# Two layer norms' inverse roots in one GpSimd instruction, and the first norm's statistics one step ahead

## The chip, the cores and the metric

The kernel runs on one core of a Trainium2 chip. The metric is the device time of one execution in microseconds; three executions of the kernel before took 194.07 to 194.81 us, median 194.49. Profiled executions come with a trace of every engine: PE (TensorE, matmuls; PEld is its loading of weights), DVE (VectorE), ACT (ScalarE), POOL (GpSimd) and SP (which issues DMAs).

## The reference

A layer of pre-norm linear attention with gate and depthwise convolution, and a small FFN in fp8, over x of shape (32, 256, 128):

```python
def _layernorm(x, axis=-1, eps=1e-05):
    m = jnp.mean(x, axis=axis, keepdims=True)
    v = jnp.var(x, axis=axis, keepdims=True)
    return (x - m) / jnp.sqrt(v + eps)

# attention on h = _layernorm(x):
q, k, v = h @ Wq.T, h @ Wk.T, h @ Wv.T      # 8 heads of 16; rope on q and k
kv   = einsum('bshd,bshe->bhde', k, v); ksum = k.sum(1); vsum = v.sum(1)
o    = (q.kv * scale + vsum) / (q.ksum * scale + seq_len) + conv5(v) + lepe_b
x    = x + (o * (h @ Wg.T)) @ Wo.T
# FFN on h2 = _layernorm(x):
y    = fp8(bf16(h2) / s_in) @ fp8(kernel / s_k) * (s_in * s_k)
out  = x + (y.astype(bf16) + bias)
```

What the change touches is the 1 / sqrt(v + eps) of both norms, which is computed on POOL as (v + eps) to the power of −0.5.

## The kernel before, in words

The 32 sequences are handled as U = 16 units of two sequences (W = 512 tokens, four tiles of 128). The kernel is a software pipeline over steps t = 0 .. 20, written out by hand: every engine has a loop over t, and in each step it works on several units at once, LN1 of unit t, the projections of unit t−1, attention of unit t−2, output projection and LN2's statistics of unit t−3, LN2's normalisation and the FFN of unit t−4. LAG = 4 is that distance. Each engine executes its list strictly in order; semaphores (wait_ge) tie the engines together.

The lists per step are:

- SP: load_x(t+1) into one of NX = 4 buffers, which from unit 4 on waits until the residual of the unit that had the buffer is done (x2_done); then store(t−4). Ahead of the loop stand the loads of x(0), the rope tables, x(1) and seven small constants.
- PE: project_qk(t−2, 1), project_v(t−1), transpose_t1(t−3), sum_v(t−2), transpose_h2(t−4), transpose_v(t−1), project_qk(t−1, 0), ffn(t−4), project_o(t−3), key_value(t−2), transpose_q(t−2), project_g(t−2), transpose_h(t), attend(t−2). transpose_v and project_qk(·, 0) wait for ACT's move_v.
- DVE: add_lepe(t−3), stats1(t) (bn_stats of x), gate(t−3), rope(t−1, 0), the first convolution tap, residual(t−3), mask_kv(t−2), stats2(t−3), two more taps, invert and divide(t−2), rope(t−1, 1). In step 0 the projections' weights are set up behind stats1(0), in step 1 the FFN's weights (set_up_ffn).
- ACT: norm2(t−4) (L328), move_v(t−1) (L276), the fp8 quantisation (L338), var_eps1(t) (L241, L242), conv_outer and conv_middle(t−1) (L288, L297), move_y(t−4) (L347), norm1(t) (L253), move_qT(t−2) (L306), var_eps2(t−3) (L316, L317), move_hT(t) (L266).
- POOL: pow1(t) (L384, L386), add_bias(t−4) (L426), final_sum(t−4) (L435), pow2(t−3) (L395, L397), sum_outer(t−2) (L419), add_rope(t−1, 0) and add_rope(t−1, 1) (L406).

A norm thus goes through three engines: DVE's bn_stats; ACT's two instructions over 128x4, which give minus the mean (nm) and the variance plus eps (ve); POOL's pow, which gives rs, and its multiplication nm · rs (nmr); and ACT's four activations of 128x128 with scale rs and bias nmr. pow2 and its product stand between stats2 of unit t−3 and norm2 of the same unit, which is the first thing that ACT does in the next step.

Of the kernel before, what the change touches and what calls it, by code (L numbers as in the profile page):

```python
# [20 lines left out]
LAG = 4  # L21
NX = 4

# [8 lines left out]
def live(u):  # L32
    return 0 <= u < U
# [12 lines left out]
def build(nc, x, wq, wk, wv, wg, wo, lepe_w, lepe_b, ffn_w, s_in, s_k, ffn_b,  # L46
          cos_c, sin_c, ident_c, mask_c, out):
    ctx = ExitStack()
    with ctx:
# [28 lines left out]
        qn = sb("qn", [P, W])  # L78
        minus_half = sb("minus_half", [P, TPU])
        eps = sb("eps", [P, 1])  # L80
# [25 lines left out]
        st2 = sb("st2", [P, 2, BPU, 6])  # L106
        ve2 = sb("ve2", [P, 2, TPU])
        nm2 = sb("nm2", [P, 2, TPU])
        rs2 = sb("rs2", [P, 2, TPU])
        nmr2 = sb("nmr2", [P, 2, TPU])  # L110
        h2 = sb("h2", [P, 2, TPU, D], BF16)
# [33 lines left out]
        ve1_done = sem("ve1_done")  # L145
        pow1_done = sem("pow1_done")
        nmr1_done = sem("nmr1_done")
        h_done = sem("h_done")
# [27 lines left out]
        ve2_done = sem("ve2_done")  # L176
        pow2_done = sem("pow2_done")
        nmr2_done = sem("nmr2_done")
        h2_done = sem("h2_done")
# [12 lines left out]
        def _(sp):  # L192
# [16 lines left out]
            for dst, src in ((cos_t[:], cos_c), (sin_t[:], sin_c)):  # L209
                sp.dma_start(dst, src).then_inc(rope_in, 16)  # L210
            load_x(1)
            for dst, src in ((conv_w[:], lepe_w.rearrange("c a k -> c (a k)")),
                             (conv_b[:], lepe_b.rearrange("(c a) -> c a", a=1)),
                             (mask[:], mask_c),
                             (fw[:], ffn_w),
                             (fb[:], ffn_b.rearrange("(a c) -> a c", a=1).broadcast_to([P, D])),
                             (sc[:, 0:1], s_in.rearrange("(a c) -> a c", a=1).broadcast_to([P, 1])),
                             (sc[:, 1:2], s_k.rearrange("(a c) -> a c", a=1).broadcast_to([P, 1]))):
                sp.dma_start(dst, src).then_inc(c_in, 16)
            for t in range(1, U + LAG):  # L220
                load_x(t + 1)
                store(t - 4)
# [4 lines left out]
        def _(act):  # L227
            for n, w in enumerate((wq, wk, wv, wg)):
                act.dma_start(w_raw[:, n], w).then_inc(w_in, 16)
            act.wait_ge(const_set, 1)  # L230
            nc.scalar.activation(scratch[:], minus_half[:, 0:1], ACT.Identity)

            def var_eps1(u):
                if not live(u):
                    return
                s = u % 2
                act.wait_ge(stats1_done, count(u))
                if u >= 2:
                    act.wait_ge(nmr1_done, count(u, 2))
                stats = st1[:, s].rearrange("p b (a k) -> p (b a) k", k=3)  # L240
                nc.scalar.activation(nm1[:, s], stats[:, :, 1], ACT.Copy, scale=-1.0)  # L241
                nc.scalar.activation(ve1[:, s], stats[:, :, 2], ACT.Identity, scale=1.0 / D,  # L242
                                     bias=eps[:, 0:1]).then_inc(ve1_done, 1)

            def norm1(u):
                if not live(u):
                    return
                s = u % 2
                act.wait_ge(nmr1_done, count(u))
                if u >= 2:  # L250
                    act.wait_ge(hT_filled, count(u, 2))
                for t in range(TPU):
                    last = nc.scalar.activation(h[:, s, t], xs[:, u % NX, t], ACT.Identity, scale=rs1[:, s, t:t + 1],  # L253
                                                bias=nmr1[:, s, t:t + 1])
                last.then_inc(h_done, 1)
# [52 lines left out]
            def var_eps2(u):  # L308
# [7 lines left out]
                nc.scalar.activation(nm2[:, s], stats[:, :, 1], ACT.Copy, scale=-1.0)  # L316
                nc.scalar.activation(ve2[:, s], stats[:, :, 2], ACT.Identity, scale=1.0 / D,  # L317
                                     bias=eps[:, 0:1]).then_inc(ve2_done, 1)

            def norm2(u):  # L320
                if not live(u):
                    return
                s = u % 2
                act.wait_ge(nmr2_done, count(u))
                if u >= 2:
                    act.wait_ge(h2T_filled, count(u, 2))
                for t in range(TPU):
                    last = nc.scalar.activation(h2[:, s, t], x2[:, u % 3, t], ACT.Identity, scale=rs2[:, s, t:t + 1],  # L328
                                                bias=nmr2[:, s, t:t + 1])
                last.then_inc(h2_done, 1)  # L330
# [19 lines left out]
            is_small = None  # L350
            for t in range(U + LAG + 1):
                if t == 4:
# [4 lines left out]
                quantise_if_small(t - 4, is_small)  # L357
                var_eps1(t)
                conv_outer(t - 1)
                conv_middle(t - 1)  # L360
                move_y(t - 4)
                norm1(t)
                move_qT(t - 2)
                var_eps2(t - 3)
                move_hT(t)

        @block.gpsimd
        def _(pool):
# [7 lines left out]

            def pow1(u):
                if not live(u):
                    return
                s = u % 2  # L380
                pool.wait_ge(ve1_done, count(u))
                if u >= 2:
                    pool.wait_ge(h_done, count(u, 2))
                nc.gpsimd.tensor_tensor(rs1[:, s], ve1[:, s], minus_half[:], ALU.pow).then_inc(pow1_done, 1)  # L384
                pool.wait_ge(pow1_done, count(u))
                nc.gpsimd.tensor_tensor(nmr1[:, s], nm1[:, s], rs1[:, s], ALU.mult).then_inc(nmr1_done, 1)  # L386

            def pow2(u):
                if not live(u):
                    return  # L390
                s = u % 2
                pool.wait_ge(ve2_done, count(u))
                if u >= 2:
                    pool.wait_ge(h2_done, count(u, 2))
                nc.gpsimd.tensor_tensor(rs2[:, s], ve2[:, s], minus_half[:], ALU.pow).then_inc(pow2_done, 1)  # L395
                pool.wait_ge(pow2_done, count(u))
                nc.gpsimd.tensor_tensor(nmr2[:, s], nm2[:, s], rs2[:, s], ALU.mult).then_inc(nmr2_done, 1)  # L397

# [48 lines left out]
        def _(dve):  # L447
# [421 lines left out]
```

## Time and profile before

| | |
|---|---|
| median of three executions | 194.49 us |
| the profiled execution | 195.21 us |
| its span in the trace | 193.4 us |
| PE busy | 162.5 us (84%) |
| DVE busy | 151.9 us (79%) |
| POOL busy | 135.6 us (70%) |
| ACT busy | 133.2 us (69%) |
| mean granted clock of TensorE | 0.95 |

The span is the time from the first to the last instruction of the trace; the execution's time is that with what lies around it. Busy shares are averages over a fill (up to about 31 us), a plateau of equal steps and a drain (from about 163 us). The granted clock is a share of TensorE's full speed.

### The profile page before, as it was taken

How to read it: one execution, taken by the hardware profiler on the slowest of the kernel's cores; microseconds unless marked ns; L12 is line 12 of the kernel's file. 1: busy time of each engine (PE TensorE's matmuls, PEld its weight loads, DVE VectorE, ACT ScalarE, POOL GpSimd, SP SyncE). 2: the span in 40 equal slices, each digit the busy share in tenths (PEclk: the TensorE clock that was granted, in tenths of full speed). 3: DMA queues.
4: the chain of work that ended last, by engine and by line, in shares of the span. 5: the costliest groups of instructions: out<-in, count | busy, mean ns of one | idle time of the engine just before them, and what ended most of it. 6: DMA issues, size and time to landing. Idle time of an engine off the chain costs nothing.

```text
span 193.4 us, 3840 instructions
## 1 busy us (share of the span) xinstructions
PE 162.5 (84%) x1125; PEld 138.5 (72%) x1125; DVE 151.9 (79%) x308; ACT 133.2 (69%) x354; POOL 135.6 (70%) x154
## 2 busy tenths in 40 slices
PE   0467659999999999999999999999999999594220
PEld 0354549888888888989898989898989888473110
DVE  1215985999999999999999999999999989845300
ACT  3437163688888979797979797979797975435150
POOL 1213081568979897989897979898979795963704
PEclk9999988999999999999999999999999999998555
DMA  5730000010303030303030303030303020110101
GB/s 138 198 99 0 0 0 0 7 54 0 108 3 110 5 108 2 108 3 110 3 108 0 112 4 108 6 106 14 98 18 96 0 58 2 54 34 23 54 0 54
DMA packets 19078, 9.71 MB, mean 50 GB/s; under 512 B 1520, under 2 KB 18800, under 8 KB 19056
## 3 DMA queue, kind: packets, MB, share of 16 engines
q1 hardware_dynamic: 18480, 9.19, 16.6%
q10 hardware_dynamic: 576, 0.26, 0.5%
q8 instruction: 10, 0.16, 0.4%
q14 instruction: 12, 0.10, 0.2%
HBM read 5.25 MB, written 4.19 MB: 49 GB/s over the span
## 4 chain that ended last, share of the span: by engine, by line
PE 76%; issue 8%; DVE 4%; POOL 4%; ACT 4%; DMA 2%; POOLq 1%; DVEq 0%; ACTq 0%
PE bank L669 13%; PE bank L770 9%; PE bank L683 8%; PE bank L728 7%; PE p_num L741 7%; PE p_num L751 7%; PE bank L692 7%; PE bank L654 4%; PE bank L702 4%; PE bank L761 4%; PE bank L713 3%; PE bank L793 2%; DMA xs<-_attn_hidden_states_dram 2%; PE bank L781 2%; POOL qk L406 1%
## 5 line engine op out<-in xcount | busy, mean ns | idle before, releaser
L406 POOL TENSOR_TENSOR qk<-rc,rs 128x512 f32<-128x512 f32 x32 | 40.2, 1276 | 12.9 <-DVE rs L524 12.9
L540 DVE SCALAR_TENSOR_TENSOR acc<-bank,conv_w,acc 128x510 f32<-128x510 f32 (+1 forms) x48 | 35.5, 739 | 1.1 <-ACT acc L297 0.5
L328 ACT ACTIVATE h<-x,nmr,rs 128x128 bf16<-128x128 f32 x64 | 26.4, 482 | 12.1 <-POOL nmr L397 12.1
L669 PE MATMUL bank<-w_qk,hT 128*128 128x256 f32 x128 | 33.8, 387 | 0.0
L426 POOL TENSOR_TENSOR yc<-yb,fb 128x512 bf16<-128x512 bf16 x16 | 18.5, 1158 | 17.5 <-ACT yb L347 17.5
L522 DVE TENSOR_TENSOR rc<-bank,cos_t 128x512 f32<-128x512 f32 x32 | 21.9, 685 | 10.1 <-PE bank L669 10.0
L253 ACT ACTIVATE h<-xs,nmr,rs 128x128 f32<-128x128 f32 x64 | 26.3, 492 | 2.0 <-POOL nmr L386 2.0
L384 POOL TENSOR_TENSOR rs<-ve,minus_half 128x4 f32<-128x4 f32 x16 | 16.3, 1018 | 15.2 <-ACT ve L242 15.2
L669 PEld LDWEIGHTS bank<-w_qk,hT 128*128 128x128 f32 x128 | 22.4, 195 | 1.8
L524 DVE TENSOR_TENSOR rs<-bank,sin_t 128x512 f32<-128x512 f32 x32 | 21.8, 680 | 0.0
L728 PE MATMUL bank<-v,qk 128*128 128x136 f32 x128 | 17.5, 280 | 3.5 <-POOL qk L406 3.5
L419 POOL TENSOR_TENSOR acc<-acc,outer 128x508 f32<-128x508 f32 x16 | 20.3, 1268 | 0.0
L395 POOL TENSOR_TENSOR rs<-ve,minus_half 128x4 f32<-128x4 f32 x16 | 16.3, 1017 | 5.2 <-ACT ve L317 4.6
L435 POOL TENSOR_TENSOR ob<-x,yc 128x512 f32<-128x512 f32 x16 | 18.6, 1160 | 1.3
L338 ACT ACTIVATE q<-bank,rsc 128x512 fp8e4<-128x512 bf16 x16 | 11.0, 687 | 12.1 <-PE bank L781 12.1
L683 PEld LDWEIGHTS bank<-w_v,hT 128*128 128x128 f32 x128 | 17.5, 200 | 2.5 <-ACT hT L266 1.8
L770 PE MATMUL bank<-w_o,oT 128*128 128x128 f32 x128 | 19.0, 294 | 0.3
L683 PE MATMUL bank<-w_v,hT 128*128 128x128 f32 x128 | 18.0, 286 | 1.0 <-ACT hT L266 0.9
L728 PEld LDWEIGHTS bank<-v,qk 128*128 128x128 f32 x128 | 16.0, 190 | 3.9 <-issue 3.9
L751 PE MATMUL p_num<-kvs,qT 128*128 128x136 f32 x128 | 17.8, 282 | 0.0
L770 PEld LDWEIGHTS bank<-w_o,oT 128*128 128x128 f32 x128 | 16.3, 199 | 1.9 <-issue 0.6
L741 PE MATMUL p_num<-w_v,hsum 128*128 128x272 f32 x64 | 17.3, 393 | 0.0
(72 smaller groups left out, 329.4 us busy)
## 6 DMA issues: line engine op xcount, KB each, us to landing
xs<-_attn_hidden_states_dram SPq DMA_DIRECT2D x16, 256.0 KB, 2.8
out_dram<-ob SPq DMA_DIRECT2D x16, 256.0 KB, 2.3
cos_t<-in_cos_dram SPq DMA_DIRECT2D x1, 256.0 KB, 4.3
sin_t<-in_sin_dram SPq DMA_DIRECT2D x1, 256.0 KB, 5.4
mask<-in_mask_dram SPq DMA_DIRECT2D x1, 68.0 KB, 3.8
w_raw<-in_L_attn_Wq_dram ACTq DMA_DIRECT2D x1, 64.0 KB, 2.7
w_raw<-in_L_attn_Wk_dram ACTq DMA_DIRECT2D x1, 64.0 KB, 3.1
ident<-in_ident_dram SPq DMA_DIRECT2D x1, 64.0 KB, 3.2
```

Source lines behind the costliest of these rows:

```text
L253: last = nc.scalar.activation(h[:, s, t], xs[:, u % NX, t], ACT.Identity, scale=rs1[:, s, t:t + 1], bias=nmr1[:, s, t:t + 1])
L328: last = nc.scalar.activation(h2[:, s, t], x2[:, u % 3, t], ACT.Identity, scale=rs2[:, s, t:t + 1], bias=nmr2[:, s, t:t + 1])
L406: nc.gpsimd.tensor_tensor(qk[:, u % 2, j].rearrange("p q t d -> p t q d"), rc[:, j].rearrange("p a h (q d) -> p (a h) q d", q=2), rs[:, j] ...
L522: nc.vector.tensor_tensor(rc[:, j], p_qk[j], cos_t[:].rearrange("p a (h d) -> p a h d", h=2), ALU.mult)
L524: nc.vector.tensor_tensor(rs[:, j], p_qk[j][:, :, ::-1, :], sin_t[:].rearrange("p a (h d) -> p a h d", h=2), ALU.mult).then_inc(rope_done[ ...
L540: nc.vector.scalar_tensor_tensor(out=part, in0=p_vT[:, :, lo + off:hi + off], scalar=conv_w[:, k:k + 1], in1=part, op0=ALU.mult, op1=ALU.a ...
L669: last = nc.tensor.matmul(p_qk[j][:, a].rearrange("p h d -> p (h d)"), hT[:, u % 3, t * P:(t + 1) * P], w_qk[:].rearrange("p a q d -> p (a ...
L683: last = nc.tensor.matmul(p_v[:, t], hT[:, u % 3, t * P:(t + 1) * P], w_v[:, 0:D], start=True, stop=True)
L728: last = nc.tensor.matmul(p_kv[:, t // TPB], qk_tile(u, 1, t), v[:, u % 3, t], start=(t % TPB == 0), stop=(t % TPB == TPB - 1))
L741: nc.tensor.matmul(p_num[:, TPB * j:TPB * (j + 1), 0:NW], hsum[:, u % 3, j:j + 1].to_broadcast([P, P]), w_v[:].unsqueeze(1).to_broadcast([ ...
L751: last = nc.tensor.matmul(p_num[:, t, 0:NW], qT[:, u % 2, t * P:(t + 1) * P], kvs[:, u % 2, t // TPB], start=False, stop=(t % TPB == TPB - 1))
L770: last = nc.tensor.matmul(p_proj[:, t], oT[:, u % 2, t * P:(t + 1) * P], w_o[:], start=True, stop=True)
```

## The change

The four small arrays of both norms (ve, nm, rs, nmr) become arrays with a further dimension of two: index 0 is LN1, index 1 is LN2, so that for one buffer the eight values of a partition lie side by side. POOL's pow1 and pow2 become invert_roots(u), which handles LN1 of unit u and LN2 of unit u−4 in one pow over 128x8 and one multiplication over 128x8; where only one of the two units exists it takes that half (128x4). It stands where pow2 stood. LN1's statistics are moved one step forward: DVE's stats1(t+1) takes stats1(t)'s place (stats1(0) runs ahead of the loop), and ACT's var_eps1(t+1) goes behind move_qT, next to var_eps2. SP loads x(t+2) in step t instead of x(t+1), x(2) is loaded ahead of the constants, and there are five x buffers. The loops of ACT and POOL start at t = −1.

```diff
-NX = 4
+NX = 5
...
-        minus_half = sb("minus_half", [P, TPU])
+        minus_half = sb("minus_half", [P, 2, TPU])
...
-        ve1 = sb("ve1", [P, 2, TPU])
-        nm1 = sb("nm1", [P, 2, TPU])
-        rs1 = sb("rs1", [P, 2, TPU])
-        nmr1 = sb("nmr1", [P, 2, TPU])
+        ve = sb("ve", [P, 2, 2, TPU])
+        nm = sb("nm", [P, 2, 2, TPU])
+        rstd = sb("rstd", [P, 2, 2, TPU])
+        nmr = sb("nmr", [P, 2, 2, TPU])
...
             load_x(1)
+            load_x(2)
...
             for t in range(1, U + LAG):
-                load_x(t + 1)
+                load_x(t + 2)
                 store(t - 4)
...
             def var_eps1(u):
...
                 if u >= 2:
-                    act.wait_ge(nmr1_done, count(u, 2))
+                    act.wait_ge(nmr_done, u - 1)
...
             def norm1(u):
...
-                act.wait_ge(nmr1_done, count(u))
+                act.wait_ge(nmr_done, u + 1)
...
             def var_eps2(u):
...
-                if u >= 2:
-                    act.wait_ge(nmr2_done, count(u, 2))
+                act.wait_ge(nmr_done, u + LAG - 1)
...
             def norm2(u):
...
-                act.wait_ge(nmr2_done, count(u))
+                act.wait_ge(nmr_done, u + LAG + 1)
...
-            for t in range(U + LAG + 1):
+            for t in range(-1, U + LAG + 1):
...
                 quantise_if_small(t - 4, is_small)
-                var_eps1(t)
                 conv_outer(t - 1)
                 conv_middle(t - 1)
                 move_y(t - 4)
                 norm1(t)
                 move_qT(t - 2)
+                var_eps1(t + 1)
                 var_eps2(t - 3)
                 move_hT(t)
...
+            def invert_roots(u):
+                s = u % 2
+                first, second = live(u), live(u - LAG)
+                if not (first or second):
+                    return
+                k = slice(0 if first else 1, 2 if second else 1)
+                if first:
+                    pool.wait_ge(ve1_done, count(u))
+                    if u >= 2:
+                        pool.wait_ge(h_done, count(u, 2))
+                if second:
+                    pool.wait_ge(ve2_done, count(u, LAG))
+                if live(u - LAG - 2):
+                    pool.wait_ge(h2_done, count(u, LAG + 2))
+                nc.gpsimd.tensor_tensor(rstd[:, s, k], ve[:, s, k], minus_half[:, k], ALU.pow).then_inc(pow_done, 1)
+                pool.wait_ge(pow_done, u + 1)
+                nc.gpsimd.tensor_tensor(nmr[:, s, k], nm[:, s, k], rstd[:, s, k], ALU.mult).then_inc(nmr_done, 1)
...
-            for t in range(U + LAG + 1):
-                pow1(t)
+            for t in range(-1, U + LAG + 1):
                 add_bias(t - 4)
                 final_sum(t - 4)
-                pow2(t - 3)
+                invert_roots(t + 1)
                 sum_outer(t - 2)
                 add_rope(t - 1, 0)
                 add_rope(t - 1, 1)
...
             is_small = None
+            stats1(0)
+            set_up_projections()
             for t in range(U + LAG + 1):
                 add_lepe(t - 3)
-                stats1(t)
-                if t == 0:
-                    set_up_projections()
+                stats1(t + 1)
```

## Rows read from the trace of the kernel before

**Rows 1.** The page: span, and busy time by engine with its share of the span.
```profile
span 193.4 us, 3840 instructions
PE 162.5 (84%) x1125; PEld 138.5 (72%) x1125; DVE 151.9 (79%) x308; ACT 133.2 (69%) x354; POOL 135.6 (70%) x154
```

**Rows 2.** Busy time of each engine: the plateau, and one step of it.
```profile
core 0: us, PE busy (x) PEld busy (x) DVE busy (x) ACT busy (x) POOL busy (x), PEclk, DMA share, GB/s
40.66:155.06 114.40, 114.30 (x843) 100.35 (x842) 110.08 (x217) 97.51 (x266) 101.35 (x109) 1.00 0.18 52
101.95:111.49 9.54, 9.54 (x71) 8.36 (x71) 9.15 (x20) 8.14 (x23) 8.33 (x10) 1.00 0.20 57
```

**Rows 3.** Timeline of a plateau step: start us, us, engine, line, op, out<-in.
```profile
101.78 1.03 PE L669 MATMUL bank<-w_qk,hT 128*128 128x256 f32 x4
...
102.85 0.69 DVE L522 TENSOR_TENSOR rc<-bank,cos_t 128x512 f32<-128x512 f32 x1 [0.29 <-PE bank L669]
...
105.66 0.76 DVE L607 BATCH_NORM_STATS2 st<-x 128x6 f32<-128x256 f32 x2
...
106.56 0.28 ACT L317 ACTIVATE ve<-st,eps 128x4 f32<-128x4 f32 x1
...
106.92 1.02 POOL L395 TENSOR_TENSOR rs<-ve,minus_half 128x4 f32<-128x4 f32 x1
...
108.02 0.20 POOL L397 TENSOR_TENSOR nmr<-nm,rs 128x4 f32<-128x4 f32 x1
...
108.25 1.65 ACT L328 ACTIVATE h<-x,nmr,rs 128x128 bf16<-128x128 f32 x4 [0.59 <-POOL nmr L397]
...
109.81 0.57 ACT L276 ACTIVATE v<-bank 128x512 f32<-128x512 f32 x1
...
110.17 0.68 DVE L578 TENSOR_TENSOR t<-bank,acc 128x512 f32<-128x512 f32 x1
...
110.83 0.42 PEld L702 LDWEIGHTS bank<-ident,v 128*128 128x128 f32 x4
```

**Rows 4.** Who waited for whom: us in total, times, longest.
```profile
ACT h L328 <- POOL nmr L397: 12.1, 16, 1.4
```

**Rows 5.** POOL's groups by shape: busy us, mean ns, idle before.
```profile
L406 POOL TENSOR_TENSOR qk<-rc,rs 128x512 f32<-128x512 f32 x32 | 40.2, 1276 | 12.9 <-DVE rs L524 12.9
...
L384 POOL TENSOR_TENSOR rs<-ve,minus_half 128x4 f32<-128x4 f32 x16 | 16.3, 1018 | 15.2 <-ACT ve L242 15.2
L395 POOL TENSOR_TENSOR rs<-ve,minus_half 128x4 f32<-128x4 f32 x16 | 16.3, 1017 | 5.2 <-ACT ve L317 4.6
L386 POOL TENSOR_TENSOR nmr<-nm,rs 128x4 f32<-128x4 f32 x16 | 3.2, 201 | 1.3
L397 POOL TENSOR_TENSOR nmr<-nm,rs 128x4 f32<-128x4 f32 x16 | 3.2, 200 | 1.3
```

**Rows 6.** Waits again: POOL's longest.
```profile
POOL yc L426 <- ACT yb L347: 17.5, 16, 4.8
```

**Rows 7.** Timeline of the fill.
```profile
9.54 0.75 DVE L513 BATCH_NORM_STATS2 st<-xs 128x6 f32<-128x256 f32 x2
9.86 0.38 ACT L266 ACTIVATE hT<-bank 128x256 f32<-128x256 f32 x1 [1.21 <-PE bank L654]
...
10.75 2.08 PE L683 MATMUL bank<-w_v,hT 128*128 128x128 f32 x8 [0.93 <-ACT hT L266]
...
16.45 0.69 DVE L522 TENSOR_TENSOR rc<-bank,cos_t 128x512 f32<-128x512 f32 x1 [6.17 <-PE bank L669]
...
23.99 0.68 DVE L524 TENSOR_TENSOR rs<-bank,sin_t 128x512 f32<-128x512 f32 x1
...
24.75 1.27 POOL L406 TENSOR_TENSOR qk<-rc,rs 128x512 f32<-128x512 f32 x1 [5.66 <-DVE rs L524]
...
26.12 1.17 PE L728 MATMUL bank<-v,qk 128*128 128x136 f32 x8 [3.55 <-POOL qk L406]
```

**Rows 8.** Timeline of SP in the fill, and ACT's first use of a constant.
```profile
6.12 0.43 SPq L219 DMA_DIRECT2D sc<-n_L_ffn_input_scale_dram  x1
6.60 0.43 SPq L219 DMA_DIRECT2D sc<-_L_ffn_kernel_scale_dram  x1
...
14.67 0.69 ACT L288 ACTIVATE outer<-bank,conv_w 128x508 f32<-128x508 f32 x1 [0.93 <-PE bank L702]
```

**Rows 9.** Timeline of PE's weight loads in steps 2 and 3.
```profile
29.01 0.18 PEld L654 LDWEIGHTS bank<-ident,h 128*128 128x128 f32 x1 [0.87 <-ACT h L253]
29.51 0.66 PEld L654 LDWEIGHTS bank<-ident,h 128*128 128x128 f32 x3 [0.32 <-issue]
...
38.97 0.14 PEld L654 LDWEIGHTS bank<-ident,h 128*128 128x128 f32 x1 [0.34 <-ACT h L253]
```

More of the change, by code:

```diff
@@ L106, in build @@
         st2 = sb("st2", [P, 2, BPU, 6])
[L107 to L110, printed above, removed]
         h2 = sb("h2", [P, 2, TPU, D], BF16)
@@ L145, in build @@
         ve1_done = sem("ve1_done")
-        pow1_done = sem("pow1_done")
-        nmr1_done = sem("nmr1_done")
+        pow_done = sem("pow_done")
+        nmr_done = sem("nmr_done")
         h_done = sem("h_done")
@@ L230, in _ @@
             act.wait_ge(const_set, 1)
-            nc.scalar.activation(scratch[:], minus_half[:, 0:1], ACT.Identity)
+            nc.scalar.activation(scratch[:], minus_half[:, 0, 0:1], ACT.Identity)
             def var_eps1(u):
@@ L238, in var_eps1 @@
                 if u >= 2:
-                    act.wait_ge(nmr1_done, count(u, 2))
+                    act.wait_ge(nmr_done, u - 1)
                 stats = st1[:, s].rearrange("p b (a k) -> p (b a) k", k=3)
-                nc.scalar.activation(nm1[:, s], stats[:, :, 1], ACT.Copy, scale=-1.0)
-                nc.scalar.activation(ve1[:, s], stats[:, :, 2], ACT.Identity, scale=1.0 / D,
+                nc.scalar.activation(nm[:, s, 0], stats[:, :, 1], ACT.Copy, scale=-1.0)
+                nc.scalar.activation(ve[:, s, 0], stats[:, :, 2], ACT.Identity, scale=1.0 / D,
                                      bias=eps[:, 0:1]).then_inc(ve1_done, 1)
@@ L252, in norm1 @@
                 for t in range(TPU):
-                    last = nc.scalar.activation(h[:, s, t], xs[:, u % NX, t], ACT.Identity, scale=rs1[:, s, t:t + 1],
-                                                bias=nmr1[:, s, t:t + 1])
+                    last = nc.scalar.activation(h[:, s, t], xs[:, u % NX, t], ACT.Identity, scale=rstd[:, s, 0, t:t + 1],
+                                                bias=nmr[:, s, 0, t:t + 1])
                 last.then_inc(h_done, 1)
@@ L312, in var_eps2 @@
                 act.wait_ge(stats2_done, count(u))
-                if u >= 2:
-                    act.wait_ge(nmr2_done, count(u, 2))
+                act.wait_ge(nmr_done, u + LAG - 1)
                 stats = st2[:, s].rearrange("p b (a k) -> p (b a) k", k=3)
-                nc.scalar.activation(nm2[:, s], stats[:, :, 1], ACT.Copy, scale=-1.0)
-                nc.scalar.activation(ve2[:, s], stats[:, :, 2], ACT.Identity, scale=1.0 / D,
+                nc.scalar.activation(nm[:, s, 1], stats[:, :, 1], ACT.Copy, scale=-1.0)
+                nc.scalar.activation(ve[:, s, 1], stats[:, :, 2], ACT.Identity, scale=1.0 / D,
                                      bias=eps[:, 0:1]).then_inc(ve2_done, 1)
@@ L327, in norm2 @@
                 for t in range(TPU):
-                    last = nc.scalar.activation(h2[:, s, t], x2[:, u % 3, t], ACT.Identity, scale=rs2[:, s, t:t + 1],
-                                                bias=nmr2[:, s, t:t + 1])
+                    last = nc.scalar.activation(h2[:, s, t], x2[:, u % 3, t], ACT.Identity, scale=rstd[:, s, 1, t:t + 1],
+                                                bias=nmr[:, s, 1, t:t + 1])
                 last.then_inc(h2_done, 1)
@@ L375, in _ @@
             pool.wait_ge(const_set, 1)
-            def pow1(u):
-                if not live(u):
+            def invert_roots(u):
+                s = u % 2
+                first, second = live(u), live(u - LAG)
+                if not (first or second):
                     return
[L380 to L397, printed above, removed]
+                k = slice(0 if first else 1, 2 if second else 1)
[10 more added lines that the diff above has]
+                nc.gpsimd.tensor_tensor(nmr[:, s, k], nm[:, s, k], rstd[:, s, k], ALU.mult).then_inc(nmr_done, 1)
             def add_rope(u, j):
```

2 lines of the change are left out of this document (removed).

## The prediction

> **What bounds the kernel now.** The page comes first. Its busy line has PE at 84% of the span, DVE at 79%, POOL at 70% [rows 1], an average over a fill, a plateau and a drain. The busy time by stretches separates them: in the 114.40 us of the plateau PE is busy 114.30 us at full granted clock, against DVE 110.08, POOL 101.35 and ACT 97.51; a single step of 9.54 us looks the same, PE busy 9.54 of it [rows 2]. So a step costs what PE's instruction stream costs, and a microsecond taken from POOL or ACT is worth nothing there by itself. What the change can do in the plateau is make some other loop longer than 9.54 us.
>
> Which loop is the next longest? The timeline of one step shows it [rows 3]. PE finishes project_qk(·,0) (L669, 101.78 + 1.03 = 102.81). DVE then works without a gap from rope (102.85) to stats2 (105.66 + 0.76 = 106.42). ACT makes the second norm's variance (106.56 + 0.28 = 106.84), POOL takes its root (106.92) and multiplies (108.02 + 0.20 = 108.22), ACT normalises LN2 (108.25 to 109.90) and then moves v (109.81 + 0.57 = 110.38), and PE may transpose v and run the next project_qk(·,0), both of which wait for that v. PE came to transpose_v only at 110.83. The loop therefore has 110.83 − 110.38 = 0.45 us of slack, less the 0.03 us that a release takes from an end to the start that waits for it (108.22 to 108.25): 0.42. The chain of waits by pairs says that it is real: ACT's LN2 normalisation waited for POOL's nmr in all 16 steps, 12.1 us in all, up to 1.4 [rows 4]. This idle time costs nothing today, and it is where the change puts its longer instruction.
>
> **The change, part by part.**
>
> *The merged pow.* Before, a step has two pows of 128x4 (1018 and 1017 ns) and two multiplications of 128x4 (201 and 200 ns) [rows 5]. After, it has one of each over 128x8, in the place of the second pair, and so inside the loop above. What the removed first pair frees (1018 + 201 = 1.2 us of POOL) lies beside PE's work and ends nothing: POOL waited for yb (17.5 us over 16 steps) before add_bias [rows 6], and ve of LN2 was ready at 106.84, 0.08 us before the pow started, so an earlier final_sum would not start it sooner [rows 3].
>
> What does a pow over 8 elements per partition cost? No row shows one. From below: nothing more than 1018 ns, if the time is the instruction's own and not its elements'; less than nothing is excluded, since it does a superset of the work. From above: 1018 ns more, if all of it goes by elements. Between them: the multiplication of the same shape on the same engine takes 201 ns, so dispatch and access are at most that, and the other 1018 − 201 = 817 ns are pow's body. An add of 128x512 takes 1276 ns [rows 5], (1276 − 201) / 508 = 2.1 ns per further element, so elements as such are cheap; pow's body is the same code over each of them. A body done element by element costs 817 / 4 = 204 ns each, and four more cost 817. I take +0.82 us: the nearest row is that of the pow itself, whose time has no other visible home than its four elements. The multiplication grows by 4 × 2.1 ns, nothing.
>
> By the Trainium skill (GPSIMD Engine Reference, section 3.1, Elementwise — side-by-side cycle accounting) tensor_tensor costs about 2.6 cycles per element at 1.2 GHz; four more elements would be an estimated 9 ns. The adds here agree with it (2.1 ns), but it is measured on add, and the 1018 ns against 201 at equal shape show that pow doesn't follow it. The same page's section 7 (Performance pitfalls for Q7 kernels) says that a dependent fp32 chain pays 4 cycles per element on the chain, which is the form in which pow's time would grow with its elements, against this change. By the first rule the sum below is 0.8, by the second about 5.6.
>
> *What the longer pow does.* In a step nmr comes 0.82 us later. ACT's LN2 normalisation ends at 109.90 + 0.82 = 110.72, v at 111.20 instead of 110.38, and PE, ready for transpose_v at 110.83, starts it at about 111.23. The step grows by 0.82 − 0.42 = 0.40 us. It doesn't heal: the next step's DVE stretch hangs from the later project_qk, and the loop's length is now 9.54 + 0.40 = 9.94 us. Both halves are live when u runs from 4 to 15, 12 times: 12 × 0.40 = 4.8 us. In the drain only the second half is there, 128x4 as before, at the same place, so from 163 us on nothing changes.
>
> Behind the waiting instruction on POOL stand sum_outer and two add_rope. They end 0.82 us later, too; sum_outer would end at about 110.3 where add_lepe wanted it at 110.17, 0.1 us of DVE time against DVE's idle of 9.54 − 9.15 = 0.39 us in a step [rows 2]. Nothing there.
>
> *var_eps1 moved.* ACT issues the same two small instructions, 0.3 us from start to start, after move_qT instead of ahead of conv_outer. conv, yb and LN1's normalisation come 0.3 us earlier, which PE doesn't feel; ACT reaches var_eps2 at the same time, when stats2 ends (106.42) [rows 3]. Zero. The merged pow now waits for var_eps1(t+1) as well, which ACT issues just ahead of var_eps2: no later.
>
> *The fill.* Here the move costs. Today ACT moves hT(0) at 9.86 as soon as PE has transposed. After the change var_eps1(1) stands ahead of move_hT(0), and it waits for stats1(1), which DVE runs after setting up the projections: 9.54 + 0.75 = 10.29. With two small ACT instructions behind it hT(0) starts near 10.65, 0.8 us late. From there the chain has no slack: project_v at 10.75 waits for hT, rope(0,0) at 16.45 for PE, then DVE is busy through the taps and the ffn set-up to rope(0,1) at 23.99, POOL adds at 24.75, PE's key_value has waited 3.55 us for it at 26.12 [rows 7]. So +0.8 us. On POOL add_rope(0,0) comes behind invert_roots(2), some 1.5 us late, but key_value needs add_rope(0,1), 7 us later. stats1(2) moves out of DVE's step 2 and stats1(3) takes its place: zero.
>
> *The loads.* x(2) is issued ahead of the seven constants, so these go one issue (0.48 us) later, and wait behind 256 KB more; the last was issued at 6.60 and is used first at 14.7, with 4 us to spare [rows 8]. In the plateau load_x(t+2) waits for x2_done(t−3) exactly as load_x(t+1) did with four buffers, is issued at the same point of the step and is needed at the same point of the next. The fifth buffer pays for the step that the load was moved forward. Zero, on SP's queue too, whose store order is the same.
>
> *Sum.* 4.8 + 0.8 = 5.6 us. The profiled execution took 195.21 us (span 193.4), 0.7 above the median of 194.49; it becomes 200.8, and the median 200.1.
>
> **Rivals.**
>
> *Pow has a fixed price* (the 1018 ns are mostly a call's own, such as tables or code fetched each time). For it: the time is constant to 10 ns wherever it stands, and adds show cheap elements. Against it: nothing in the trace shows what the fixed part would be. Any growth below 0.42 us is swallowed by the slack. Only the fill is left: 194.49 + 0.8 = 195.3.
>
> *Pow grows in part* (a pipelined body: some latency once, the rest per element). With growth of 0.5 to 0.7 us: 12 × 0.08 to 0.28 = 1.0 to 3.4, and 0.8: 196.3 to 198.7.
>
> *Faster: LN1 leaves the fill's critical path.* PE's weight loads waited for LN1's h for 0.87 us before 29.01 and 0.34 before 38.97 [rows 9], because ACT's conv and norm stood behind var_eps1, and this behind a late stats1. The move takes that away: −1.2 us, 193.3. It decides if pow's growth is under 0.42 us and if hT(0)'s delay is absorbed. Against it: the other three transposes of that group started at 29.51 for another reason, so little of the 0.87 was PE's.
>
> That the change doesn't do what it says is not to be expected: the instructions are counted off.
>
> **Numbers.** Chances: pow by the element 0.57 (199.1 to 201.1: the slack may be off by 0.08 us a step either way), in part 0.12, fixed 0.23, faster 0.08. If all 1018 ns doubled, the upper bound: 12 × (1.02 − 0.42) + 0.8 = 8.0, 202.5. The range 194.9 to 201.6 takes in the fixed case and all but the top of the upper bound; the likeliest case's own is 199.1 to 201.1. About 0.5% (1 us) is what a measurement can tell from no change: slower 0.69, same 0.23 (the fixed case, 0.8 us, just under it), faster 0.08.
>
> **What would show it.** POOL's pow over 128x8 at 1.84 us; LN2's normalisation waiting 1.3 to 1.4 us for nmr; PE, without waits before, waiting for ACT's v or h2 by 0.3 to 0.4 us at transpose_v; steps of 9.94 us; hT(0) starting at 10.65. It is wrong if the pow stays near 1.0 us, or if the step stays 9.5 with a pow of 1.8, which would mean slack that I haven't seen.

## The result, and the profile after

The changed kernel is slower: 199.38 us median of four runs (198.36 to 200.25) against 194.65 for the kernel before, ratio 1.0246 (95% interval 1.019 to 1.0302). The forecast was 200.1 us, range 194.9 to 201.6. Its profiled execution took 198.36 us, 1.0 below its median. All medians here leave out one execution of the kernel "split, LN1's root next" below, which took 297.52 us at a mean granted clock of 0.58.

The page after, span and busy time by engine (before: [rows 1]):

```profile
span 196.6 us, 3818 instructions
PE 165.2 (84%) x1125; PEld 137.9 (70%) x1125; DVE 153.5 (78%) x308; ACT 134.4 (68%) x354; POOL 128.6 (65%) x130
```

POOL works 7.0 us less, and nobody is faster for it. One plateau step after, from one transpose_v to the next (columns as in [rows 2]):

```profile
103.21:113.15 9.94, 9.79 (x71) 8.29 (x71) 9.25 (x19) 8.22 (x22) 7.86 (x8) 1.00 0.19 54
```

The step takes 9.94 us, and PE now has gaps. POOL's groups by shape after (before: [rows 5]):

```profile
L385 POOL TENSOR_TENSOR rstd<-ve,minus_half 128x8 f32<-128x8 f32 x12 | 19.8, 1648 | 12.0 <-ACT ve L311 12.0
...
L385 POOL TENSOR_TENSOR rstd<-ve,minus_half 128x4 f32<-128x4 f32 x8 | 8.1, 1017 | 18.9 <-ACT ve L237 17.4 <-ACT ve L311 1.5
L387 POOL TENSOR_TENSOR nmr<-nm,rstd 128x8 f32<-128x8 f32 x12 | 2.4, 203 | 0.9
```

The wide pow takes 1648 ns, 0.63 us more than a narrow one; two narrow ones took 2035. The wide multiplication costs nothing more. The timeline of the loop in a step after (before: [rows 3]):

```profile
103.70 1.03 PE L658 MATMUL bank<-w_qk,hT 128*128 128x256 f32 x4
...
104.77 0.69 DVE L511 TENSOR_TENSOR rc<-bank,cos_t 128x512 f32<-128x512 f32 x1 [0.50 <-PE bank L658]
...
107.57 0.76 DVE L596 BATCH_NORM_STATS2 st<-x 128x6 f32<-128x256 f32 x2
...
108.36 0.21 ACT L310 ACTIVATE nm<-st 128x4 f32<-128x4 f32 x1 [0.18 <-DVE st L596]
...
108.48 0.28 ACT L311 ACTIVATE ve<-st,eps 128x4 f32<-128x4 f32 x1
...
108.99 1.65 POOL L385 TENSOR_TENSOR rstd<-ve,minus_half 128x8 f32<-128x8 f32 x1 [0.68 <-ACT ve L311]
...
110.72 0.20 POOL L387 TENSOR_TENSOR nmr<-nm,rstd 128x8 f32<-128x8 f32 x1
...
110.95 1.66 ACT L322 ACTIVATE h<-x,nmr,rstd 128x128 bf16<-128x128 f32 x4 [1.47 <-POOL nmr L387]
...
112.52 0.58 ACT L271 ACTIVATE v<-bank 128x512 f32<-128x512 f32 x1
...
113.14 0.42 PEld L691 LDWEIGHTS bank<-ident,v 128*128 128x128 f32 x4 [0.25 <-ACT v L271]
113.15 0.66 PE L691 MATMUL bank<-ident,v 128*128 128x128 f32 x4
```

Read it as a loop: from the end of project_qk (104.73) to the start of the next transpose_v (113.15) each row starts as soon as the work above it is done (DVE works without a gap from rc at 104.77 to the end of stats2 at 108.33), and no row has slack. Three things in it differ from [rows 3]. The pow is 0.63 us longer. It starts 0.23 us behind ve's end (108.76 to 108.99), where it was 0.08. And PE, which waits for v now, needs 0.49 us from the start of transpose_v to the start of project_qk (113.15 to 113.64), where it took 0.45 (110.88 to 111.33). Together 0.63 + 0.15 + 0.04 = 0.82, less the 0.42 us of slack, is 0.40; this step took 9.94 where the one of [rows 2] took 9.54, and the mean step of the plateau grew from 9.52 to 9.94.

The waits by pairs after, with ACT's from 12.1 us before to 22.4 [rows 4], and PE's two in 13 or 14 steps where it had them in 2, outside the plateau:

```profile
ACT h L322 <- POOL nmr L387: 22.4, 16, 1.5
...
PEld bank L770 <- ACT h L322: 11.5, 14, 5.3
...
PEld bank L691 <- ACT v L271: 4.0, 13, 1.0
```

**Where the 4.7 us went.** The start of transpose_v(2) is 34.57 us before and 33.79 after; that of transpose_v(14) 148.89 and 152.93, of transpose_v(15) 158.39 and 162.39; the spans end at 193.4 and 196.6. So these two profiles differ by −0.78 in the fill, +4.78 in the plateau and −0.80 in the drain, 3.2 in all. That the plateau's 4.78 is also the difference of the medians (4.73) is partly chance, since the fill and the drain vary between executions. In the profile of before the granted clock was 0.50 between 28 and 30 us and 0.87 between 170 and 180, after it was 1.00 in both stretches. The drain, from transpose_v(15) to the end, took 34.1 to 34.3 us in the three profiles where the granted clock stayed at 1.00 up to 185 us (both of the changed kernel, and the one with its waits reordered), and 34.5 to 35.1 in nine of the ten where it was 0.50 from 180 to 185 us; the tenth is the 128x8 ballast below. More on the fill below.

The fill after, down to key_value(0) (before: [rows 7]):

```profile
9.26 1.41 DVE L502 BATCH_NORM_STATS2 st<-xs 128x6 f32<-128x256 f32 x4
10.04 0.21 ACT L236 ACTIVATE nm<-st 128x4 f32<-128x4 f32 x1 [1.47 <-DVE st L502]
...
10.34 0.36 ACT L261 ACTIVATE hT<-bank 128x256 f32<-128x256 f32 x1
...
19.64 1.27 POOL L396 TENSOR_TENSOR qk<-rc,rs 128x512 f32<-128x512 f32 x1
...
20.34 0.65 DVE L456 CAST identb<-ident 128x128 bf16<-128x128 f32 x1
...
27.02 1.17 PE L717 MATMUL bank<-v,qk 128*128 128x136 f32 x8 [1.99 <-POOL qk L396]
```

hT(0) waits behind var_eps1(1), as forecast, and starts at 10.34 instead of 9.86. It is less late than the 10.65 forecast, since DVE came to stats1(1) 0.28 us sooner than before. A second 0.43 us was not forecast: DVE's cast of ident, 0.22 us before, took 0.65 beside POOL's add_rope(0,0), which stands behind LN1's root now; the add ended at 20.91 and the cast at 20.99. key_value(0) starts 0.90 us late.

### The profile page after: what moved, and what is told of

The parts are those of the page before. It is cut to its first block, busy times and chain, and to the rows that moved or that the text cites. A ratio compares the mean times of both kernels' runs of the same rounds, so it can differ in the third digit from the quotient of the medians.

```text
span 196.6 us, 3818 instructions
## 1 busy us (share of the span) xinstructions
PE 165.2 (84%) x1125; PEld 137.9 (70%) x1125; DVE 153.5 (78%) x308; ACT 134.4 (68%) x354; POOL 128.6 (65%) x130
## 4 chain that ended last, share of the span: by engine, by line
PE 23%; DVE 20%; issue 19%; POOL 17%; ACT 15%; DMA 2%; POOLq 1%; ACTq 1%; DVEq 0%
POOL rstd L385 12%; ACT h L322 7%; PE bank L658 7%; PE bank L691 5%; DVE st L596 5%; DVE acc L529 5%; ACT v L271 3%; DVE rs L513 3%; DVE kvs L540 3%; DMA w_raw<-in_L_attn_Wg_dram 2%; PE bank L672 2%; ACT ve L311 2%; DVE x L585 2%; POOL nmr L387 2%; PE bank L717 2%
## 5 line engine op out<-in xcount | busy, mean ns | idle before, releaser
L385 POOL TENSOR_TENSOR rstd<-ve,minus_half 128x8 f32<-128x8 f32 (+1 forms) x20 | 27.9, 1395 | 30.9 <-ACT ve L237 17.4
L322 ACT ACTIVATE h<-x,nmr,rstd 128x128 bf16<-128x128 f32 x64 | 26.5, 486 | 22.4 <-POOL nmr L387 22.4
L658 PE MATMUL bank<-w_qk,hT 128*128 128x256 f32 x128 | 34.7, 395 | 0.0
L248 ACT ACTIVATE h<-xs,nmr,rstd 128x128 f32<-128x128 f32 x64 | 26.5, 494 | 1.5 <-POOL nmr L387 1.5
L672 PEld LDWEIGHTS bank<-w_v,hT 128*128 128x128 f32 x128 | 18.4, 209 | 2.8 <-ACT hT L261 1.9
L672 PE MATMUL bank<-w_v,hT 128*128 128x128 f32 x128 | 18.8, 294 | 1.5 <-ACT hT L261 1.5
L759 PE MATMUL bank<-w_o,oT 128*128 128x128 f32 x128 | 17.9, 283 | 0.2
L740 PEld LDWEIGHTS p_num<-kvs,qT 128*128 128x128 f32 x128 | 15.9, 190 | 1.3 <-ACT qT L301 1.3
L681 PE MATMUL bank<-hT,w_g 128*128 128x512 f32 x32 | 16.4, 594 | 0.0
L759 PEld LDWEIGHTS bank<-w_o,oT 128*128 128x128 f32 x128 | 15.5, 191 | 1.0 <-DVE oT L577 0.4
```

Of the source, the lines that this page charges most:

```text
L385: nc.gpsimd.tensor_tensor(rstd[:, s, k], ve[:, s, k], minus_half[:, k], ALU.pow).then_inc(pow_done, 1)
L658: last = nc.tensor.matmul(p_qk[j][:, a].rearrange("p h d -> p (h d)"), hT[:, u % 3, t * P:(t + 1) * P], w_qk[:].rearrange("p a q d -> p (a ...
L672: last = nc.tensor.matmul(p_v[:, t], hT[:, u % 3, t * P:(t + 1) * P], w_v[:, 0:D], start=True, stop=True)
L740: last = nc.tensor.matmul(p_num[:, t, 0:NW], qT[:, u % 2, t * P:(t + 1) * P], kvs[:, u % 2, t // TPB], start=False, stop=(t % TPB == TPB - 1))
L759: last = nc.tensor.matmul(p_proj[:, t], oT[:, u % 2, t * P:(t + 1) * P], w_o[:], start=True, stop=True)
```

## The experiments

Medians of each, with the kernel before run on the same chip; a step is the distance of two transpose_v in the plateau.

```
kernel                        median us   before   ratio (95%)              step us
changed kernel, again          199.68     193.94   1.028  (1.021-1.035)      9.93
split, LN1's root next         197.82     194.05   1.020  (1.016-1.025)      9.79
split, LN1's root last         195.35     193.94   1.006  (1.003-1.010)      9.52
before, LN2's pow 128x8        198.56     194.05   1.023  (1.018-1.028)      9.78
before, LN2's pow 128x6        194.12     193.87   1.003  (0.999-1.007)      9.52
changed, waits reordered       199.55     194.05   1.031  (1.025-1.036)      9.88
changed, one wait fewer        199.97     193.87   1.033  (1.029-1.038)      9.83
changed, hT(0) first           198.80     193.94   1.026  (1.020-1.033)      9.93
before, early set_up_ffn       190.66     193.94   0.984  (0.979-0.988)      9.52
split last + both fill edits   190.62     193.87   0.986  (0.982-0.989)      9.52
merged + both fill edits       195.78     194.11   1.010  (1.005-1.015)      9.93
```

**Undo the merging.** LN2's root and LN1's as two pows of 128x4, with semaphores of their own; the statistics stay one step forward.

```diff
-                invert_roots(t + 1)
+                invert_root2(t - 3)
+                invert_root1(t + 1)
                 sum_outer(t - 2)
```

> The changed kernel with its one pow over 128x8 taken apart again: LN2's root (128x4) where the merged one stood, LN1's (128x4) right behind it. The statistics stay one step forward, with five x buffers. Theory (the longer pow and its wait in the loop from stats2 to move_v are the whole plateau loss): the wait of PE for ACT's v goes, steps return from 9.94 to 9.5 us, and 12 x 0.42 = 5.0 us come back: 194.4 us or a little less, level with the kernel before. Rival (the forward move costs in the plateau, by its order on ACT, the waits for LN1's variance, or the loads): steps stay near 9.9 us and the time near 199.

Neither: 197.82 us, steps of 9.79. The pow is short again and ACT waits for nmr as before (11.7 us in all), but something new ends last. DVE in that kernel:

```profile
110.51 0.68 DVE L521 TENSOR_TENSOR rs<-bank,sin_t 128x512 f32<-128x512 f32 x1
111.69 0.69 DVE L575 TENSOR_TENSOR t<-bank,acc 128x512 f32<-128x512 f32 x1 [0.50 <-POOL acc L416]
112.30 0.75 DVE L510 BATCH_NORM_STATS2 st<-xs 128x6 f32<-128x256 f32 x2
112.97 0.67 DVE L585 TENSOR_TENSOR oT<-bank,t 128x512 f32<-128x512 f32 x1
```

add_lepe waits 0.50 us for sum_outer, which stands behind 1.2 us of LN1's root on POOL; gate (112.97) and PE's project_o come behind it. So POOL's tail has a deadline too. The next run moves LN1's root behind it.

```diff
                 invert_root2(t - 3)
-                invert_root1(t + 1)
                 sum_outer(t - 2)
                 add_rope(t - 1, 0)
                 add_rope(t - 1, 1)
+                invert_root1(t + 1)
```

> The split kernel (two pows of 128x4, statistics one step forward), with LN1's root at the end of POOL's step, behind sum_outer and both add_rope, instead of ahead of them. Theory (the 0.27 us a step that the first split still lost are DVE's add_lepe waiting for sum_outer, which stood behind 1.2 us of LN1's root, with gate and project_o behind it): that wait goes, steps fall from 9.79 to 9.52 us, 12 x 0.27 = 3.2 us; against the kernel before only the fill's +0.5 to +0.9 is left: 194.6 to 195.2 where it takes 194.2. Rival (the forward move itself costs a plateau step, through ACT's order or the loads): steps stay near 9.8 us.

Steps of 9.52 us, 195.35 us. The plateau of the kernel before is back, with the statistics still one step forward and five buffers: the forward move costs nothing there. On POOL the order is that of the kernel before again, where LN1's root also follows both add_rope; moved forward are the loads, DVE's statistics and ACT's variance. What is left is 1.4 us against before (ratio 1.003 to 1.010); forecast were 0.5 to 0.9. In the two profiles only the fill differs: transpose_v(2) starts at 35.01 us against 34.57, plateau and drain agree to 0.13 us. The executions lie in groups by their mean granted clock, and the medians within a group are 194.01 against 193.21 at 0.973 to 0.975 and 195.54 against 194.11 at 0.955 to 0.958, so the loss is 0.8 to 1.4. In this kernel the cast took 0.22 us again, as POOL was idle beside it. The three placements side by side, all with the forward move: roots apart and LN1's last, 9.52; apart and adjacent, 9.79, with sum_outer late; together, 9.94, with nmr of LN2 late. The next run has the wide pow without anything else of the change.

**The wide pow alone.** The kernel before with four constant columns added to LN2's ve; the multiplication stays 128x4.

```diff
-        ve2 = sb("ve2", [P, 2, TPU])
-        rs2 = sb("rs2", [P, 2, TPU])
+        ve2 = sb("ve2", [P, 2, 2 * TPU])
+        rs2 = sb("rs2", [P, 2, 2 * TPU])
```

> The kernel before, in which LN2's pow alone is widened from 128x4 to 128x8 by four constant columns that nobody reads; LN1's pow stays, nothing is moved. Theory (the price of a wide pow in that place suffices): the pow takes 1.65 us; beyond a slack of 0.42 us a step grows by 0.63 - 0.42 = 0.21 us, 9.75 us, 12 times = 2.5 us, and three or four steps of the drain, where LN2 is on the path without slack, pay 0.63 us each: 2 us more; 198.5 to 199.5 us. Rival (slack is larger than counted, the loss comes from the move): steps stay at 9.5 us and the time under 197.

Right: 198.56 us, steps of 9.77 to 9.78. Its timeline, with the pow 0.08 us behind ve and PE waiting for v:

```profile
107.26 0.28 ACT L317 ACTIVATE ve<-st,eps 128x4 f32<-128x4 f32 x1
107.62 1.65 POOL L396 TENSOR_TENSOR rs<-ve,minus_half 128x8 f32<-128x8 f32 x1 [0.35 <-ACT ve L317]
...
111.76 0.42 PEld L703 LDWEIGHTS bank<-ident,v 128*128 128x128 f32 x4 [0.26 <-ACT v L276]
```

0.63 + 0.04 − 0.42 = 0.25, and 9.52 + 0.25 = 9.77. Here all 16 pows of LN2 are wide, also in the drain: the 13 steps from transpose_v(2) to transpose_v(15) took 126.99 us against 123.82 before, and the drain 36.27 against 35.01, 3.2 and 1.3 of the 4.5 us by which the medians differ. With two columns instead of four the growth should vanish in the slack.

> The kernel before with LN2's pow widened from 128x4 to 128x6 by two constant columns that nobody reads (the run with four had 9.78 us steps and 198.56 us). Theory (a slack of 0.38 to 0.42 us in the loop from stats2 to move_v; 157 ns per element): the pow takes 1.32 us, 0.31 more, which the slack swallows; steps stay at 9.52 us, and only the drain pays, about 3 x 0.31 = 0.9 us: 194.6 to 195.2 where the kernel before takes 193.9. Rival (POOL's longer step costs in proportion): half of the loss of 128x8, 2.3 us, steps of 9.65.

It does: the pow took 1332 ns, steps stayed at 9.52, and the time, 194.12, can't be told from that of the kernel before. A dose below the slack costs a plateau step nothing, a dose above it costs the excess in every step. The 0.9 us forecast for the drain didn't come: it took 34.83 us against 35.01, and the medians differ by 0.25.

**What a pow costs.** Behind the last step of the kernel before, one pow after another, then multiplications.

> The kernel before with POOL instructions behind its last step, each waiting for the one before: pow over 4, 4, 1, 2, 3, 5, 6, 7, 8, 12, 16, 32, 64 elements per partition, then multiplications over 1, 4, 8, 64. Linear theory (fixed part plus equal price per element; 1018 ns at 4 and 1648 ns at 8 give 157.5 ns each and 388 ns fixed): 545 ns at 1, 1.18 us at 5, 2.9 us at 16, 10.5 us at 64. Rival (a body over groups of four): about 1.02 us from 1 to 4, 1.65 us from 5 to 8, then a step per group. Rival (the code is fetched on each change of operation): the second pow of 4, right behind a pow, is shorter than 1018 ns.

POOL's groups in that kernel (the groups of 4, 8, 1 and 64 mix pow and multiplication, with the multiplication at 0.2 to 0.3 us):

```profile
L453 POOL TENSOR_TENSOR pout<-pin,pex 128x32 f32<-128x32 f32 x1 | 5.4, 5426 | 0.1
...
L453 POOL TENSOR_TENSOR pout<-pin,pex 128x16 f32<-128x16 f32 x1 | 2.9, 2900 | 0.1
L453 POOL TENSOR_TENSOR pout<-pin,pex 128x12 f32<-128x12 f32 x1 | 2.3, 2267 | 0.1
...
L453 POOL TENSOR_TENSOR pout<-pin,pex 128x7 f32<-128x7 f32 x1 | 1.5, 1477 | 0.1
L453 POOL TENSOR_TENSOR pout<-pin,pex 128x6 f32<-128x6 f32 x1 | 1.3, 1322 | 0.1
L453 POOL TENSOR_TENSOR pout<-pin,pex 128x5 f32<-128x5 f32 x1 | 1.2, 1165 | 0.1
...
L453 POOL TENSOR_TENSOR pout<-pin,pex 128x3 f32<-128x3 f32 x1 | 0.8, 848 | 0.1
...
L453 POOL TENSOR_TENSOR pout<-pin,pex 128x2 f32<-128x2 f32 x1 | 0.7, 704 | 0.1
```

Linear: (5426 − 704) / 30 = 157 ns per element, and 704 − 2 × 157 = 390 ns fixed. There are no groups of four, and a pow right behind a pow is no shorter (the two of 128x4 took 1012 ns in the mean). These pows had one constant input, 1.7; with the kernels' own data 128x4 and 128x8 took 1017 and 1648 ns, on the same line. Joining two pows can save 0.39 us of POOL at most, and puts 157 ns per added element where the joint one stands.

**The late start.**

```diff
-                if first:
-                    pool.wait_ge(ve1_done, count(u))
-                    if u >= 2:
-                        pool.wait_ge(h_done, count(u, 2))
-                if second:
-                    pool.wait_ge(ve2_done, count(u, LAG))
+                if first and u >= 2:
+                    pool.wait_ge(h_done, count(u, 2))
                 if live(u - LAG - 2):
                     pool.wait_ge(h2_done, count(u, LAG + 2))
+                if first:
+                    pool.wait_ge(ve1_done, count(u))
+                if second:
+                    pool.wait_ge(ve2_done, count(u, LAG))
```

> The changed kernel with the four waits ahead of the merged pow in another order: those that are long satisfied (h_done, h2_done) first, then ve1_done, then ve2_done last. Theory (the 0.16 us by which the pow starts later behind ve2, 0.24 instead of 0.08, is POOL's sequencer working through waits after the release): the start falls back to 0.08 us behind ve2, steps from 9.94 to 9.78 us, time down by 12 x 0.16 = 1.9 us. Rival (the late start is the wide instruction's own, or goes by the count of waits and not by their order): steps stay at 9.94 and the time within 0.5 us of the changed kernel.

Between the two: the start falls from 0.23 to 0.17 us behind ve, steps from 9.94 to 9.88, and not to 9.78. In the next run the order is the old one and the wait for ve1_done is left out where ve2_done is waited for.

> The changed kernel without POOL's wait for ve1_done where it also waits for ve2_done, which ACT releases later in its order. Theory (each wait ahead of the merged pow beyond two costs it 0.08 us, since 1 or 2 waits gave a start 0.08 us behind ve2, 3 waits 0.16 and 4 waits 0.24): the start comes 0.16 us behind ve2, steps fall from 9.94 to 9.86 us, about 1 us in all: 198.7 where the changed kernel takes 199.7. Rival (the order of the waits alone matters): start and step unchanged.

Its timeline:

```profile
117.31 0.28 ACT L311 ACTIVATE ve<-st,eps 128x4 f32<-128x4 f32 x1
...
117.73 1.65 POOL L386 TENSOR_TENSOR rstd<-ve,minus_half 128x8 f32<-128x8 f32 x1 [0.41 <-issue]
```

0.14 us behind ve, steps of 9.83. So both order and number count, and the width doesn't: the wide pow of the ballast kernel, behind two waits, started at 0.08. The 0.15 us go with the waits; that POOL's sequencer works them off behind the last release is the reading that fits, and how they split isn't settled. Neither gain shows in the medians (199.55 and 199.97 where the changed kernel has 199.38 and 199.68), which by the plateau alone should be 0.7 and 1.3 us lower. Four of the five executions with one wait fewer had a mean granted clock of 0.949 to 0.951 and took 199.6 to 200.3, the fifth had 0.958 and took 197.69; the changed kernel's eight had 0.956 to 0.976. So the stretches outside the plateau can hide either gain.

**The fill.** The changed kernel with ACT's hT(0) ahead of var_eps1(1):

```diff
+                if t == 0:
+                    move_hT(0)
                 var_eps1(t + 1)
                 var_eps2(t - 3)
-                move_hT(t)
+                if t != 0:
+                    move_hT(t)
```

> The changed kernel with one exception in step 0: ACT moves hT(0) ahead of var_eps1(1) instead of behind it. Theory (this order is the fill's loss): hT(0) starts at about 9.8 us instead of 10.34, PE's key_value(0) at 26.5 instead of 27.0, and the time falls by 0.5 us against the changed kernel; DVE's cast of ident still takes 0.65 instead of 0.22 us, since it falls beside POOL's add_rope(0,0), which stands behind LN1's root of unit 2. Rival (the fill's chain has slack at hT(0)): key_value(0) stays at 27.0.

hT(0) started at 9.85, key_value(0) at 26.51, as forecast, and the cast took 0.63 us. The median, 198.80, is 0.9 below the changed kernel on that chip, in the direction expected but within the spread of the two (198.5 to 199.2 and 198.3 to 200.4). To test that this chain sets the fill, the kernel before got DVE's set_up_ffn ahead of rope(0,0):

```diff
                 if t == 1:
+                    set_up_ffn()
                     dve.wait_ge(rope_in, 32)
...
-                if t == 1:
-                    set_up_ffn()
```

> The kernel before with nothing of the change, but DVE's set_up_ffn (3.5 us, today between the taps of unit 0 and rope(0,1)) run ahead of rope(0,0), where DVE waits for PE until 16.45. It tests that the chain through hT(0), rope(0,0), set_up_ffn, rope(0,1) and key_value(0) sets the fill, so that what stands on it costs or gives its full length. Theory: rope(0,1) and key_value(0) come 3.5 us earlier (22.6 instead of 26.1) and the time falls by about that, less what then limits PE itself: 190.6 to 192. Rival (the fill is set elsewhere, by PE's own work or the loads): under 1 us.

190.66 us: 3.3 us faster than the kernel before, and faster than both. PE in that kernel reaches key_value(0) at 23.77, with no wait ahead of it; forecast was 22.6, and PE's own work ends last now:

```profile
22.90 1.03 PE L668 MATMUL bank<-w_qk,hT 128*128 128x256 f32 x4
23.77 1.09 PE L727 MATMUL bank<-v,qk 128*128 128x136 f32 x8
```

With both edits on the split kernel, and then on the merged one:

> Three edits on the changed kernel: the root split with LN1's half at the end of POOL's step, hT(0) moved ahead of var_eps1(1), and DVE's set_up_ffn ahead of rope(0,0). What is left of the change is the forward move with its fifth x buffer. Theory (a plateau step is PE's 9.52 us whatever LN1's place, and the fill is now PE's own, too): level with the kernel before plus the early set_up_ffn, 190.7 us, within 0.5. Rival (the forward move is worth something where LN1's h was late in steps 1 to 3): 0.5 to 1.2 us less, 189.5 to 190.2.

190.62 us, level with 190.66 (ratios 0.986 and 0.984 to the kernel before on the same chip): within the intervals the forward move is worth nothing once the fill is mended, and costs nothing.

> The changed kernel with its merged pow and its four waits as they are, but hT(0) ahead of var_eps1(1) and DVE's set_up_ffn ahead of rope(0,0). Beside the run that had the same two edits and the roots split (190.62 us) it differs in the merging alone. Theory (the merging costs 0.42 us in each of 12 plateau steps and nothing else): steps of 9.94 us, 190.6 + 4.8 to 5.0 = 195.4 to 195.6 us. Rival (part of the changed kernel's loss was its late, low-clocked fill): under 194.5 or, if the fill hid part of it, over 196.

195.78 us, steps of 9.93. The merging costs 195.78 − 190.62 = 5.2 us between the two chips, or 1.67 + 3.25 = 4.9 against the kernel before on each; 12 × 0.42 = 5.0. It is the same with the fill mended as without.

**The changed kernel again**, beside these:

> The changed kernel once more, as the yardstick of the runs beside it on this chip. Theory: steps of 9.94 us again, key_value(0) at 27.0 us, median 199 to 200. The fill can differ from profile to profile by TensorE's rate between 17 and 32 us: either it is slow early and waits about 2 us for key_value(0), or it is fast early, waits about 4 us and has a granted clock of 0.5 right behind.

199.68 us, with steps of 9.93 and key_value(0) at 27.59: DVE came to stats1(1) at 9.86, 0.60 us later than in its first profile, and hT(0) and all behind it followed. The weights' DMA sets this: PE's first transposes waited for it until 7.50 us here and 6.89 there. With var_eps1(1) ahead of it hT(0) started anywhere from 10.02 to 10.95 in six profiles; with hT(0) ahead, as before, from 9.81 to 9.92 in eight.

## Why the prediction was right, point by point

The bound and the loop: right. PE set the step at 9.52 us, the loop from project_qk through stats2, LN2's root, norm2 and move_v was next, and its slack was 0.42 us: a pow 0.31 us longer cost no time in a step, one 0.63 us longer did.

*The merged pow*: the size was off. The sum took +0.82 us for four more elements, by putting all of the 817 ns beyond a multiplication to the elements. Measured is +0.63: of the 817, 190 are fixed (390 less the multiplication's 200) and 157 ns go to each element. The rival of growth in part, with 0.5 to 0.7 us, was the true one for the pow itself. By it the step would have grown by 0.21 us and the time been near 198. The slip was to take the multiplication's 201 ns as the most that a pow could have fixed. The prediction's figure of 5.6 us by the rule of the Trainium skill (GPSIMD Engine Reference, section 7, Performance pitfalls for Q7 kernels) isn't what that rule gives: 4 cycles per element at 1.2 GHz would be an estimated 13 ns for four elements and leave the sum at 0.8. The 157 ns per element follow neither of the two rules.

*What the longer pow does*: the step grew by 0.42 us, as forecast with 0.40, but by luck, through a sum that happened to close: 0.19 us too much for the pow was made good by 0.15 us of late start with four waits and 0.04 us of PE restarting, which the prediction didn't have. It took the pow's start as 0.08 us behind ve whatever is waited for. The prediction saw that the merged pow also waits for var_eps1 and said "no later", which holds for the data and not for the pow's start.

*Count of steps*: 12, right (4.78 us in the profiles).

*var_eps1 moved, loads*: right; the split kernel with LN1's root last has the old step.

*POOL's tail* ("Nothing there"): right in the changed kernel, but close. sum_outer ended at 112.15 where add_lepe started at 112.25, and the first split, with 1.2 us instead of 0.63 ahead of sum_outer, lost 0.27 us a step by it.

*The fill*: hT(0) and its mechanism right, +0.48 at hT(0) where +0.8 was said, and with the 0.43 us of the cast beside POOL's add, which it didn't foresee, key_value(0) came 0.90 late. How much of that reaches the plateau isn't a fixed number. Profiles with the granted clock at 1.00 behind key_value(0) reach transpose_v(2) at 33.64 and 33.65 (the ballast kernels, whose fill is that of before), at 33.79 (the changed kernel) and at 33.29 to 33.47 (three of its variants: hT(0) first, one wait fewer, the first split): no loss that can be told. In others, with the clock at 0.50 for a while there, it is 34.57 for the kernel before, 35.01 for the split with LN1's root last, 35.49 for the reordered waits and 36.05 for the second profile of the changed kernel. The medians fit with a few tenths: 199.38 against 194.65 and 199.68 against 193.94 are 4.7 and 5.7 us apart, of which 12 × 0.42 = 5.0 are plateau. What is left of them for the fill, −0.3 and 0.7, is less than the +0.8 forecast; the 0.8 to 1.4 of the split with LN1's root last are as much or more.

*The rival of a faster fill* was partly there: the ballast kernels' transpose_h(2) waited 0.43 us for LN1's h, the changed kernel's didn't. In the profiles at full clock it ate the later key_value(0) wholly or nearly, and in the three variants 0.2 to 0.4 us more than that. It won nothing in the medians.

## What to carry to other kernels

Before two small operations of different stages are joined into one, look where the joint one will stand: it takes the place of the more urgent, longer by the other's elements. Saving 7.0 us of busy time on POOL, which wasn't the bound, was worth nothing here, while the length of an instruction inside the next-longest loop is paid from the moment the loop's slack is used up; work out that slack from the timeline (here 110.83 − 110.38 − 0.03) before changing anything. And look at the fill separately: set-up work moved into an idle stretch was worth 3.3 us, where this change had nothing to win in the plateau.

## What the runs showed of the hardware

- POOL's pow cost 390 ns plus 157 ns per element of a partition, from 2 to 32 elements; an add costs 2.1 ns per element (1276 ns at 128x512). The Trainium skill (GPSIMD Engine Reference, section 3.1, Elementwise — side-by-side cycle accounting) has about 2.6 cycles per element for tensor_tensor, measured on add, an estimated 2.2 ns at 1.2 GHz; that holds for the add here and not for the pow.
- POOL's pow with four waits ahead of it started 0.23 us behind the last release, with the last released put last 0.17, with three waits 0.14, with two 0.08, though the others had been satisfied before.
- DVE's cast of 128x128 f32 to bf16 took 0.63 to 0.72 us while POOL was adding (six profiles: two of the changed kernel, the two with other waits, the one with hT(0) first, the first split) and 0.22 with POOL idle (four: the kernel before, both ballast kernels, the split with LN1's root last). In each of the six the cast started 0.55 to 0.64 us ahead of the add's end and ended 0.08 us behind it (20.99 and 20.91 in the changed kernel): it looks held until the add is done, not slowed. The Trainium skill (GPSIMD Engine Reference, section 8, Key points) says that POOL shares its SBUF interfaces with VectorE and that they contend when VectorE is in a two-port mode or has two SBUF inputs; the cast has one input, and no run here tells its mode.
- In the fill the same matmuls ran at two rates in different profiles of kernels alike up to there: four passes of transpose_h(1) took 0.66 us in the profile of before (17.61) and 1.12 in that of the kernel with the 128x8 ballast (17.61), both with a granted clock of 1.00. In the first PE then waited 3.55 us for key_value(0), and the granted clock was 0.50, 1.2 GHz, between 28 and 30 us; in the second it waited 1.47 us and the clock stayed at 1.00, 2.4 GHz. Two profiles with the slow early rate had a fall to 0.50 as well, after waits of 2.43 and 2.79 us (the split with LN1's root last, the second of the changed kernel). The length of the early passes is that of the lower level, which the view doesn't show there: four passes of project_qk took 1.91 us at 14.42 and 1.03 at 18.10 in the profile of before, both at a granted clock of 1.00, and project_g, 1.02 in the plateau, took 1.91 at 27.80, at 0.50. Executions of one kernel spread by it: 17 of the kernel before on one chip took 192.9 to 193.3 us at a mean granted clock of 0.973 to 0.975 (seven), 193.8 to 194.4 at 0.955 to 0.958 (eight) and 194.9 and 195.7 at 0.948 and 0.949. What chooses the first rate was not tried.
